# Moving the scan tile of slot c, between the second and the third m-tile, to the end of each routed body

## The reference

```
state = state * exp(delta[..., None] * A) + (delta * u)[..., None] * B[:, None, :]
y_t   = einsum('ben,bn->be', state, C)
...
x = x + tanh(g_xattn) * ssm(ctx, layernorm(x), ...)
x = x + tanh(g_ffn)   * moe(layernorm(x), ...)
```

## Time and profile before

| | us |
|---|---|
| median of 3 runs | 1623.14 |
| lowest and highest | 1621.38, 1624.61 |
| the profiled execution, its own time | 1615.96 |
| its span, first to last instruction | 1614.1 |
| mean granted clock of PE | 0.978 |

### The profile page before, as it was taken

How to read it: one execution, slowest core, us unless ns; L and a number is a source line. 1 busy time by engine, 2 the same in 40 slices (tenths; PEclk the granted TensorE clock), 3 DMA queues, 4 the chain that set the end, 5 groups by cost and what they waited for, 6 DMA issues and landing times.

```text
span 1614.1 us, 19148 instructions
## 1 busy us (share of the span) xinstructions
PE 1509.3 (94%) x6440; PEld 1146.2 (71%) x6440; DVE 1160.2 (72%) x1638; ACT 659.8 (41%) x1035; POOL 743.1 (46%) x536
## 2 busy tenths in 40 slices
PE   5678799988888899999999999999999999999999
PEld 3334377766666667778777777777777777887787
DVE  6899867988899867688888856888888653333333
ACT  6555345544454434543444345434444321211111
POOL 3589421887878702287777401676777000000000
PEclk9799899998999999999999999999999999999999
DMA  7799538698878873889789645899897458778882
GB/s 257 260 334 313 208 114 273 212 317 291 280 269 286 282 257 143 246 294 296 249 254 276 230 150 200 261 301 276 265 283 231 172 191 261 223 220 247 252 244 97
DMA packets 144945, 395.99 MB, mean 245 GB/s; under 512 B 25456, under 2 KB 66672, under 8 KB 129616
## 3 DMA queue, kind: packets, MB, share of 16 engines
q1 hardware_dynamic: 124624, 342.07, 63.5%
q10 hardware_dynamic: 20224, 52.70, 11.3%
HBM read 306.30 MB, written 68.16 MB: 232 GB/s over the span
## 4 chain that ended last, share of the span: by engine, by line
PE 59%; DVE 17%; POOL 9%; issue 5%; ACT 5%; DMA 4%; ACTq 1%; SPq 1%; DVEq 0%; POOLq 0%
PE b_u L819 14%; PE b_g L819 14%; PE b_u L913 8%; POOL ring L1516 5%; PE b_q L913 4%; PE b_q L867 3%; DVE ring L1613 3%; PE b_g L913 3%; PE b_g L885 3%; DVE tt L1587 2%; DMA raw<-in_gu 2%; PE b_g L852 2%; PE b_u L852 2%; DVE ring L1619 2%; POOL gm L1461 2%
## 5 line engine op out<-in xcount | busy, mean ns | idle before, releaser
L1516 POOL TENSOR_TENSOR ring<-du,rep 128x512 f32<-128x512 f32 x256 | 348.5, 1369 | 136.8 <-DVE du L1695 106.3
L819 PE MATMUL b_g<-xnb,gm 128*128 128x512 f32 (+1 forms) x1440 | 352.6, 394 | 0.9 <-DVE xnb L1590 0.9
L819 PE MATMUL b_u<-xnb,gm 128*128 128x512 f32 (+1 forms) x1440 | 349.4, 392 | 0.8 <-DVE xx L1587 0.8
L1525 POOL TENSOR_TENSOR yx<-yx,ring 128x512 f32<-128x512 f32 x192 | 266.2, 1387 | 152.1 <-DVE ring L1619 151.5
L1613 DVE TENSOR_TENSOR_SCAN ring<-b_a,ring 128x512 f32<-128x512 f32 x256 | 310.8, 1214 | 16.0 <-ACT b_a L1060 14.3
L819 PEld LDWEIGHTS b_g<-xnb,gm 128*128 128x128 f32 (+1 forms) x1440 | 256.0, 179 | 78.9 <-issue 8.8
L819 PEld LDWEIGHTS b_u<-xnb,gm 128*128 128x128 f32 (+1 forms) x1440 | 257.4, 179 | 73.1 <-DVE xx L1587 2.0
L1587 DVE SCALAR_TENSOR_TENSOR tt<-tt,b_g 128x512 f32<-128x512 f32 (+1 forms) x120 | 82.0, 684 | 197.4 <-ACT tt L1060 197.2
L1060 ACT ACTIVATE b_a<-delta,cs 128x512 f32<-128x512 f32 x256 | 173.3, 681 | 80.0 <-DVE ring L1613 75.8
L913 PE MATMUL b_u<-dwt,hhl 128*128 128x512 f32 (+1 forms) x720 | 193.7, 399 | 3.0 <-DVE daw_s L1590 1.7
L1060 ACT ACTIVATE tt<-b_g 128x512 f32<-128x512 f32 (+1 forms) x120 | 71.2, 593 | 284.4 <-PE b_u L852 241.2
(11 more groups left out here) (248 smaller groups left out, 1923.9 us busy)
## 6 DMA issues: line engine op xcount, KB each, us to landing
gm<-scr_gm SPq DMA_DIRECT2D x64, 1024.0 KB, 9.3
dwt<-scr_dw SPq DMA_DIRECT2D x32, 1536.0 KB, 6.7
rep<-bc_d ACTq DMA_DIRECT2D x64, 512.0 KB, 7.0
gm<-scr_gm SPq DMA_DIRECT2D x32, 768.0 KB, 5.4
scr_gm<-gm SPq DMA_DIRECT2D x20, 1024.0 KB, 7.2
dqt<-scr_dq SPq DMA_DIRECT2D x25, 640.0 KB, 9.1
qat<-scr_qa SPq DMA_DIRECT2D x25, 512.0 KB, 9.2
awt<-aw_h ACTq DMA_DIRECT2D x48, 256.0 KB, 4.7
```

Of the source, the lines that this page charges most:

```text
L819: i = mm(out_b[0:IW[m], :], w, v, start=(n == 0), stop=(n == 11 and not is_routed(s)))
L1516: v.tensor_tensor(ring_at(nb, T), du[:, T % 4, :], rep[:, N % NREP, 0], ALU.mult).then_inc(pool_dbu, 1)
L1525: v.tensor_tensor(yd, yd, ring[:, T % NRING], ALU.add).then_inc(pool_y, 1)
```

## The change

The tile of slot c goes. In bodies 1 to 6 the tiles of the slots behind it move up by one slot, and f gets two. In body 1, which has ten tiles, the extra one moves from slot a to slot d. In body 0, c had two tiles; one goes to d and one to f. The same table serves DVE and ACT. POOL's and SP's programs and the number of tiles of a body stay as they are.

```
         SLOTS = ("a", "h0", "b", "h1", "c", "h2", "d", "e", "f")
-        FIRST_BODY = {"h0": 1, "b": 1, "h1": 1, "c": 2, "h2": 1, "d": 1, "e": 1, "f": 1}
+        FIRST_BODY = {"h0": 1, "b": 1, "h1": 1, "h2": 1, "d": 2, "e": 1, "f": 2}
+        LATER_BODY = {"a": 1, "h0": 1, "b": 1, "h1": 1, "h2": 1, "d": 1, "e": 1, "f": 2}

         def tiles_in(e, slot):
             t = first_tile(e)
             for name in SLOTS:
-                n = FIRST_BODY.get(name, 0) if e == 0 else 2 if name == "a" and e == 1 else 1
+                n = (FIRST_BODY if e == 0 else LATER_BODY).get(name, 0) + (1 if name == "d" and e == 1 else 0)
```

## The result

The changed kernel takes 1652.27 us (median of 4 runs, 1651.99 to 1655.97), the kernel before 1622.26 us beside it (1620.27 to 1624.61): a ratio of 1.0198, 95% interval 1.0176 to 1.022. The change makes the kernel slower by some 2%, 30 us between the medians. The prediction was 1658 us, range 1630 to 1682.

What follows compares the result with a forecast made beforehand. The prediction took batch 0 to be decided by POOL's in-order queue up to qb's scale, then DVE's tile and first add_down. Queue 21, clock 14 and batches 1 and 2 at 0 gave +35 us: 1658 us, range 1630 to 1682.

Steps and rivals of the forecast that it cites:

- 504.9 and 525.7: Body 5 of batch 0: forecast times of the third m-tile's first product (506.64 before) and first add_down (522.00 before).
- POOL wins its delay back: Rival, slower but little: each body loses only 0.1 to 1.8 us, stands too short for the clock; 1630 us, chance 0.15.
- the third m-tile decides: Rival, faster: freeing PE's 21.3 us of waits in batch 0 gives 1589 us at best, likelier 1606; chance 0.08.
- no change: Rival: the sum of DVE's work sets batch 0's bodies, so order moves only its idle time; 1623 us, chance 0.07.
- The queue term: Batch 0: later qb from POOL plus slot f's second tile, 3.6 us in seven bodies, less cover: 21 us.
- The clock term: Batch 0: PE stands before line 819's twelve matmuls drop its clock, 2 us in each of seven bodies: 14 us.
- 12.7 us spent: Bodies 1 to 6 of batch 0 before the change: clock loss, worked out as 253.2 x 0.05.
- cap of 16 us: Whole kernel: clock cost limit from the skill's under 1% of span, some 13 already spent; sum then about 24 us.
- Batches 1 and 2: No pieces, POOL not queued: up to +7 us from lost cover, -5 from body 3's excess, taken as 0.
- cover of 1.5 us in body 2: Batch 1: first add_down ended 1.5 us before PE came; if lost, up to 0.5 us in each of 14 bodies.
- The sum: Whole kernel: 21 + 14 + 0 = +35 us, 1651 us against the profiled execution, 1658 us on the median.
- The signs that were named: Batch 0: line 885 under 8 us, line 819 3 to 7 per body, qb waits over 2 in most, six bodies 280.

Runs made afterwards that it cites:

- x6: Changed kernel with qb's scale on POOL moved right behind the low half of gm1 in bodies 1 to 6 of batch 0: 1626.99 us.
- x8: Kernel before, slot c's tile moved to slot a in bodies 2 to 6 of batch 0 and body 3 of batches 1 and 2: 1606.6 us.
- x3: Changed kernel with, in batch 0, the c_mult of slot h1's tile moved back into slot c, ahead of the third m-tile: 1638.33 us.
- x4: Changed kernel with, in batch 0, the first of slot f's two tiles ahead of qb's low half (DVE) and rounding (ACT): 1643.78 us.
- x1: Kernel before with the new table of slots only in the bodies of batch 0: 1646.62 us, ratio 1.0165.
- x2: Kernel before with the new table of slots only in batches 1 and 2: 1625.05 us, ratio 1.0025.

## Why the prediction was right, and which of its steps were off

**The direction and the mechanism** held: the gain was taken where the page's waits point, and the price came by the queue that the chain pointed to. The third m-tile's product and the first add_down of body 5 lie 19.8 us apart (526.89 to 546.68), 15.4 us before; the prediction's 504.9 and 525.7 gave 20.8. POOL's queue passed its delay on unshortened (11.2 against 11.3 us), so "POOL wins its delay back" was wrong, and "the third m-tile decides" with it. Against "no change" stands x6: 23 us for the place of one instruction, at equal work. The kernels x8 and the changed one lie 46 us apart, yet POOL's busy time in them is 737.5 and 742.9 us and DVE's 1151.4 and 1155.5 us. The Trainium skill (Perfetto Trace Analysis, Identifying the Most-Contended Engine) has the engine with the highest occupancy optimized first. These occupancies alone do not tell the two kernels apart.

**The queue term** was 21 us. PE stood still 22.5 us longer in batch 0. Its two halves, per body 1.9 us of feeding POOL late and 1.8 us of a second tile behind the wait, were measured as 13 and 9 us for seven bodies (x3, x4, clock included). The forecast that PE would stand 7 us behind body 5 came out at 5.83. The gain ahead of it had a part that the prediction did not have: of the 1.56 us by which the second wait at the third m-tile shrank, 1.55 us is one DVE instruction, the low half of the hidden rows, which took 2.23 us beside POOL before and takes 0.68 us now (last section).

**The clock term** was 14 us, 2 us for each of seven new stands. That is what the openings cost: the twelve matmuls behind the seven stands took 34.8 us instead of 20.6, 14.2 us more. Yet all 1115 matmuls of the seven bodies together ran only 8.9 us longer. The step left out that the kernel before already paid for the lower level inside its bodies (the earlier trace rows is one place), and that this price would move: the matmuls away from the openings took 5.3 us less than before. That 14 was so near to 14.2 has some luck in it, for a stand of a given length does not always cost the same: after 2.87 us the twelve took 4.60 us in the changed kernel, after 2.90 us they took 3.01 us in x4.

The working of "12.7 us spent" multiplied the missing granted clock with the whole stretch, and so counted time in which PE stood. PE's busy time is the better measure. Two of the six bodies before, 5 and 6, ran at a granted clock of 1.00:

```profile
481.90:522.50 40.60, 35.84 (x159) 25.90 (x158) 37.21 (x42) 19.75 (x30) 35.49 (x24) 1.00 0.87 288
522.50:563.10 40.60, 35.58 (x159) 26.29 (x160) 34.69 (x42) 17.34 (x26) 33.87 (x23) 1.00 0.80 273
```

At their rate the 950 matmuls take 213 us (an estimate). So the lower clock cost the six bodies about 10 us before (223.8 us of PE) and 18 us after (231.2 us).

The six bodies alone thus lose 0.6% of the span before and 1.1% after. The Trainium skill (TensorE: Matmul & The Clock Gate, Part 1: The HAM clock gate) puts the ramp's price at under 1% of a typical kernel's span. By these estimates the changed kernel passes that in the six bodies alone. The prediction's cap of 16 us, worked out from that figure, left 3 us for the clock term, the rows gave 14, and 8.9 were measured.

**Batches 1 and 2** were taken at 0, with bounds of -5 and +7. They cost 4 us. Both single effects were named: body 3 gave back its 2.4 us, and the cover of 1.5 us in body 2 did go, so that four openings of each batch have PE stand 0.5 to 0.7 us, and the four bodies run 0.8 to 1.6 us longer. Taking them to cancel was the error; the second is the larger.

**The sum.** From the profiled executions the change costs 36.5 us (1652.51 against 1615.96), forecast 35. The terms came out as 22.5 + 8.9 + 3.8 = 35.2 where 21 + 14 + 0 was written, so their misses cancel: that the sum is so near is luck. Between the medians the change costs 30 us, since the profiled execution of before lay 6 us under its median and that of the changed kernel did not. The granted clock goes with such differences. Of the 51 executions of the kernel before that were timed beside the experiments, the 18 with a mean granted clock of 0.977 or more have a median of 1616.6 us and the 22 with 0.973 or less one of 1621.8 us; the profiled one had 0.978. Putting the sum on the median carried this scatter into the 1658. It lies in the terms too. The profiles of x1 and x2, with the new and the old table in batch 0, give the same stretch once more:

```profile
309.26:628.41 319.15, 263.57 (x1114) 191.58 (x1115) 249.16 (x308) 136.49 (x205) 217.85 (x145) 0.93 0.75 253
```

```profile
307.57:599.13 291.56, 257.48 (x1115) 189.78 (x1115) 248.50 (x302) 135.27 (x202) 213.66 (x143) 0.94 0.81 277
```

Here PE stands still 21.5 us longer and its matmuls run 6.1 us longer, where the first pair gave 22.5 and 8.9.

**The signs that were named.** Line 885's waits, forecast under 8 us, were 8.2 us. Line 819 waited 2.9 to 5.8 us at the opening of each of bodies 1 to 6, forecast 3 to 7. DVE waited 29.7 us for qb, in seven waits. The six bodies took 279.6 us, forecast 280, and their granted clock fell to 0.91. Only batches 1 and 2 did not all keep their 33.5 us.

## What to carry to other kernels

A tile that is moved on one engine moves the inputs of every in-order queue that it feeds; follow the queue to its next fixed piece, and count what is queued behind the wait for that piece. The longest wait in a table names the engine that stands, not the price of freeing it: here 13 us less of one wait cost 28 us more of another. Before work is moved to the end of a loop, look for a place ahead of it that feeds the queues as early as before; and where a piece is late, moving the piece inside its own queue may be worth as much as undoing the change.

## What the runs showed of the hardware

The low half of the third m-tile's hidden rows took 2.23 us in body 5 before and 0.68 us after, though it is the same instruction. From the timelines of POOL and DVE, first the kernel before at that point, then the changed kernel at the low half of daw_s in the same body:

```profile
509.00 2.36 POOL L1461 TENSOR_TENSOR gm<-raw,gm 128x1024 fp32r<-128x1024 f32 x1
...
509.67 2.23 DVE L1590 TENSOR_TENSOR hhl<-tt,hhl 96x512 fp32r<-96x512 f32 x1
```

```profile
535.74 1.28 POOL L1526 TENSOR_TENSOR yx<-yx,ring 128x512 f32<-128x512 f32 x1
...
535.85 1.72 DVE L1591 TENSOR_TENSOR daw_s<-dawf,daw_s 64x512 fp32r<-64x512 f32 x1
```

Both DVE instructions read both operands from SBUF and begin inside an instruction of POOL; they end 0.54 and 0.55 us after POOL's end. Such low halves (hidden rows, awt, daw_s; 300 to 640 us) took 0.69 us where no POOL instruction ran beside them. Where one began inside a POOL instruction, more than 0.1 us after its start and more than 0.1 us before its end, it ended 0.54 to 0.55 us behind that instruction, in all 15 cases before and all 12 after. So 0.55 of its 0.69 us lay behind POOL's end. The Trainium skill (SBUF — State Buffer, Who interferes with whom) says that a DVE instruction with two SBUF inputs contends with a GpSimd instruction that reads SBUF, that the port pair which they share is an exclusive lock, and that the order of issue decides who blocks. The trace agrees, with these numbers. POOL's low halves of gm, its long pieces, met the low half of the hidden rows in this way four times before and never in the changed kernel; there they met that of awt twice. So the order on DVE also decides which of its instructions pays for POOL's.
